# Attention stage of a four-layer transformer block: another written order of the work on all four engines

## The chip, the cores and the metric

The kernel runs on one core of one Trainium2 chip, in one launch. The metric is the device time of the core in microseconds (us), the median of three runs. The engines are PE (TensorE, matrix products; its weight loads are listed as PEld), DVE (VectorE), ACT (ScalarE), POOL (GpSimd) and SP (SyncE, here only the issuing of transfers). Each engine works through its own instructions in the order in which they are written; between engines, semaphores decide.

## The reference

Four layers, each an attention-like part plus a feed-forward-like part on a normalised input, over 4096 rows of 128 values (16 sequences of 256 rows as the kernel lays them out). Only the first layer, called L0 in the kernel, is touched:

```python
# x: 16 sequences x 256 rows x 128;  16 heads of 8
xn = layernorm(x)
q, k, v = heads(xn @ Wq.T + bq), heads(xn @ Wk.T + bk), heads(xn @ Wv.T + bv)
att = softmax(where(causal, q @ k.T / sqrt(8), -inf))
attn = (att @ v) @ Wp.T + bp
ffn = (fp8(xn / s_in) @ fp8(kernel / s_k)) * (s_in * s_k) + bias
x = x + attn + ffn
```

The other layers (a chunked linear attention with a low-rank feed-forward, an attention with a routing tree, a state-space block with six layers of local attention) follow in stages of their own and are the same in both kernels.

## The kernel before

The program has five stages, L0, L1, L2, L3a and L3f, with a barrier of all engines between two of them. L0 works on one sequence of 256 rows at a time, in a software pipeline: the loop at its end runs over rounds k, and in round k each engine runs its list of calls (the last lines of `pe`, `act`, `dve` and `pool`), each call for its own sequence (k - 2 to k + 5). What a list says is the order on that engine. Every call waits by semaphores for its inputs and for its buffers to be free.

For one sequence the steps are: statistics of the rows (`stats`, `moments`, DVE), their logarithm and root (`ln`, `root`, ACT), the normalised rows (`normed`, POOL), turned by PE (`tx`, L299) and copied out by ACT (`xt`). From these PE makes queries and keys (`qk`, L307), which ACT writes out masked by head (`masked`, L489), and values (`vp`, L317), to which DVE adds a bias (`value`). DVE rounds a copy to eight-bit floats in five steps of two instructions (`cast`, `quant` 0 to 4, L191 to L209) for the product of the feed-forward part (`fyp`, L328), which goes on to `scaled` (DVE), `biased`, `ffn` and `keep` (POOL).

The scores of the 16 heads are made twice. In six blocks S0 to S5 (`scores`, L342 to L354) they are made with queries on the partitions, and DVE takes their maxima (`top`, L607, L609). PE turns the maxima (`turn_max`, MX, L366) and DVE lowers the queries by them (`lower`, L629). Then the scores are made again in six blocks T0 to T5 with keys on the partitions (`turned`, L382, L387), ACT takes the exponential (`exponent`, L498), DVE masks (`kept`, L622; 512 elements a partition for blocks 0 to 3, 1024 for 4 and 5), and PE multiplies with the values (`values`, L404, L407). ACT copies the result out (`out`, L507), PE sums (`sl`, L417), ACT takes logarithm and inverse (`logarithm`, `inverse`), POOL multiplies (`shared`, L704), PE projects (`project`, L426) and DVE adds to x (`residual`, L636).

S blocks and T blocks use the PSUM banks 0 to 3 as two pairs in turn, in the fixed order of `RING`: S0, T0, S1, T1, ... S5, T5, MX. So S1 waits until the maximum of S0 has been read, T1 until the exponential of T0 is done, and so on (`wait_pair`). T blocks in round k are of sequence k, S blocks of sequence k + 1. Between two neighbours of this ring other products of PE may stand.

After each round `between` may issue a piece of a later stage's set-up, on whichever engine that needs (`MADE_AT` names the rounds 1 to 7 in which it does for L1, L3a and L3f among others). These instructions stand on each engine behind what the round has issued there and ahead of the next round.

Of the kernel before, what the change touches and what calls it, by code (L numbers as in the profile page):

```python
# [13 lines left out]
NSEQ, SEQ = 16, 256  # L14
# [36 lines left out]
class Kernel:  # L51
# [77 lines left out]
    def L0(self):  # L129
# [152 lines left out]
        def seq(s):  # L282
            return 0 <= s < NSEQ
# [5 lines left out]
        def pe(k):  # L289
# [121 lines left out]
            def sl(s):  # L411
                if not seq(s):
                    return
                p.wait_ge(*o_in.at(s))
                if s:
                    p.wait_ge(*x_done.at(s - 1))
                p.matmul(PS[:, 7, :], lsel[:, :], ob[:, :], start=True, stop=True).then_inc(l_mm.sem)  # L417
# [10 lines left out]

            scores(k + 1, 1)
            turned(k, 1)  # L430
            sl(k - 1)
# [5 lines left out]
            qk(k + 2)  # L437
            scores(k + 1, 4)
            turned(k, 4)
            fyp(k + 1)  # L440
            scores(k + 1, 5)
            turned(k, 5)
            vp(k + 2)
            project(k - 1)
            turn_max(k + 1)
            values(k, 0)
            values(k, 1)
            scores(k + 2, 0)
            turned(k + 1, 0)
            values(k, 2)  # L450

        def act(k):
# [70 lines left out]
            out(k - 1)  # L523
            exponent(k, 1)
            logarithm(k - 1)
            exponent(k, 2)
            xt(k + 2)
            ln(k + 3)
            inverse(k - 1)
            exponent(k, 3)  # L530
            exponent(k, 4)
            root(k + 3)
            masked(k + 2, 0)
            exponent(k, 5)
            masked(k + 2, 1)
            exponent(k + 1, 0)

        def dve(k):
# [98 lines left out]

            quant(k + 1, 4)
            residual(k - 2)
            top(k + 1, 1)  # L640
            kept(k, 0)
            moments(k + 3, 1)
            top(k + 1, 2)
            value(k + 1)
            stats(k + 4, 0)
            kept(k, 1)
            top(k + 1, 3)
            cast(k + 2)
            quant(k + 2, 0)
            stats(k + 4, 1)  # L650
            top(k + 1, 4)
            scaled(k + 1)
            quant(k + 2, 1)
            kept(k, 2)
            top(k + 1, 5)
            quant(k + 2, 2)
            kept(k, 3)
            kept(k, 4)
            quant(k + 2, 3)
            moments(k + 4, 0)  # L660
            lower(k + 1)
            kept(k, 5)
            top(k + 2, 0)

        def pool(k):
# [40 lines left out]
            shared(k - 1)  # L706
            normed(k + 3, 0)
            normed(k + 3, 1)
            biased(k + 1)
            keep(k - 1)  # L710
            ffn(k + 1)
# [14 lines left out]
        for k in range(-2, NSEQ + 2):  # L726
            pe(k)
            act(k)
            dve(k)
            pool(k)  # L730
            self.between(0, k)
# [2553 lines left out]
```

## Time and profile before

| | us |
|---|---|
| runs (median, lowest, highest) | 4755.88, 4755.16, 4768.18 |
| profiled execution, its own time | 4755.88 |
| its span | 4754.6 |
| busy over the span: PE, DVE, ACT, POOL | 4446.8, 3757.2, 3404.6, 3668.2 |
| TensorE's mean granted clock | 0.983 of full speed |

The span is the time from the first to the last instruction of the profile. Busy times are sums over the whole program; L0 is its first 427 us, a little under a tenth. In the timeline an entry merges neighbouring instructions of one line: its start, the time to the end of the last, the operation, and in brackets how long the engine was idle just before and who ended that. Entries of PE overlap by about 0.1 us, since matmuls are pipelined, so the time that a step takes on PE is read from its start to the next start.

### The profile page before, as it was taken

How to read it: one execution, taken by the hardware profiler on the slowest of the kernel's cores; microseconds unless marked ns; L12 is line 12 of the kernel's file. 1: busy time of each engine (PE TensorE's matmuls, PEld its weight loads, DVE VectorE, ACT ScalarE, POOL GpSimd, SP SyncE). 2: the span in 40 equal slices, each digit the busy share in tenths (PEclk: the TensorE clock that was granted, in tenths of full speed). 3: DMA queues.
4: the chain of work that ended last, by engine and by line, in shares of the span. 5: the costliest groups of instructions: out<-in, count | busy, mean ns of one | idle time of the engine just before them, and what ended most of it. 6: DMA issues, size and time to landing. Idle time of an engine off the chain costs nothing.

```text
span 4754.6 us, 138457 instructions
## 1 busy us (share of the span) xinstructions
PE 4446.8 (94%) x56800; PEld 3022.2 (64%) x56800; DVE 3757.2 (79%) x5226; ACT 3404.6 (72%) x6108; POOL 3668.2 (77%) x1951
## 2 busy tenths in 40 slices
PE   7998999988887899999999999999999999999997
PEld 5776778864443566666666666666666666666665
DVE  6885466649998787888778888888888888878885
ACT  3555755547775677777778777877778787777875
POOL 2222344449997998989889999999998999989993
PEclk9999999989999999999999999999999999999999
DMA  2000000003331222223223222232323322322222
GB/s 79 2 2 2 2 1 1 1 39 165 154 143 74 66 67 56 66 73 70 64 57 74 69 66 62 67 73 64 70 61 73 72 58 68 75 67 63 59 66 52
DMA packets 164379, 290.50 MB, mean 61 GB/s; under 512 B 44063, under 2 KB 61350, under 8 KB 159654
## 3 DMA queue, kind: packets, MB, share of 16 engines
q1 hardware_dynamic: 162310, 281.40, 22.7%
q8 instruction: 453, 7.42, 0.7%
q14 instruction: 176, 1.44, 0.1%
q10 hardware_dynamic: 1440, 0.24, 0.0%
HBM read 90.16 MB, written 2.62 MB: 20 GB/s over the span
## 4 chain that ended last, share of the span: by engine, by line
PE 42%; DVE 12%; issue 7%; ACT 5%; POOL 1%; DMA 0%; SPq 0%; ACTq 0%; DVEq 0%; POOLq 0%
PE ps L2562 15%; PE ps L2575 6%; PE ps L2591 5%; PE ps L2618 5%; PE ps L2630 4%; PE ps L2672 3%; PE ps L2604 2%; DVE L3f_sm L2996 2%; DVE ps L2982 2%; DVE L3f_sm L3016 2%; DVE L3f_ss L2955 2%; DVE L3f_raw L2972 1%; DVE L3f_mx L2988 1%; ACT L2779 1%; ACT L3f_gg L2871 1%
## 5 line engine op out<-in xcount | busy, mean ns | idle before, releaser
L3155 POOL TENSOR_TENSOR L3f_t<-L3f_raw,L3f_rot 128x1024 f32<-128x1024 f32 x384 | 999.3, 2603 | 268.3 <-DVE L3f_raw L2972 268.2
L2562 PE MATMUL ps<-L3f_wqkv,all_z 128*128 128x512 f32 x2304 | 1147.0, 607 | 13.4 <-DVE L3f_raw L2972 7.8
L3172 POOL TENSOR_TENSOR L3f_raw<-L3f_raw,L3f_t 128x1024 f32<-128x1024 f32 x384 | 990.4, 2590 | 7.5
L3164 POOL TENSOR_TENSOR L3f_raw<-L3f_raw,L3f_rot 128x1024 f32<-128x1024 f32 x384 | 910.8, 2377 | 15.1
L2972 DVE TENSOR_TENSOR L3f_raw<-ps,L3f_ri 128x512 f32<-128x512 f32 x768 | 498.1, 685 | 287.9 <-ACT L3f_ri L2781 284.9
L2771 ACT ACTIVATE L3f_sqr<-ps 128x512 f32<-128x512 f32 x768 | 453.9, 598 | 174.3 <-PE ps L2562 171.3
L2955 DVE TENSOR_REDUCE L3f_ss<-L3f_sqr 128x8 f32<-128x512 f32 x768 | 509.2, 677 | 74.2 <-ACT L3f_sqr L2771 68.3
L2562 PEld LDWEIGHTS ps<-L3f_wqkv,all_z 128*128 128x128 f32 x2304 | 392.1, 192 | 253.0 <-issue 209.9
L2575 PEld LDWEIGHTS ps<-all_ident,L3f_raw 128*128 128x128 f32 x3072 | 366.6, 141 | 287.0 <-issue 248.5
L2575 PE MATMUL ps<-all_ident,L3f_raw 128*128 128x128 f32 x3072 | 472.1, 276 | 18.2 <-DVE L3f_gg L3038 7.4
L2618 PEld LDWEIGHTS ps<-L3f_pT,L3f_vw 128*64 128x64 f32 x12288 | 378.2, 139 | 97.0 <-issue 90.3
L2618 PE MATMUL ps<-L3f_pT,L3f_vw 128*64 128x64 f32 x12288 | 405.2, 225 | 7.2 <-ACT L3f_pT L2822 5.0
L2822 ACT ACTIVATE L3f_pT<-ps 64x1024 f32<-64x1024 f32 x384 | 389.4, 1014 | 17.2 <-PE ps L2604 12.6
L2805 ACT ACTIVATE L3f_kT<-ps 128x512 f32<-128x512 f32 x384 | 229.4, 597 | 197.9 <-PE ps L2575 194.3
L2630 PE MATMUL ps<-L3f_oT,L3f_wo 128*128 128x256 f32 x1536 | 351.5, 382 | 5.2 <-ACT L3f_oT L2831 3.6
L3016 DVE TENSOR_TENSOR L3f_sm<-L3f_sm,L3f_sl 128x1024 f32<-128x1024 f32 x192 | 348.5, 1815 | 0.1
L2591 PE MATMUL ps<-L3f_kT,L3f_qT 64*32 64x64 f32 x24576 | 300.7, 226 | 50.9 <-issue 37.1
L2591 PEld LDWEIGHTS ps<-L3f_kT,L3f_qT 64*32 64x32 f32 x24576 | 264.4, 105 | 118.3 <-issue 88.5
L2630 PEld LDWEIGHTS ps<-L3f_oT,L3f_wo 128*128 128x128 f32 x1536 | 290.5, 192 | 66.4 <-issue 24.6
L2982 DVE TENSOR_TENSOR ps<-ps,L3f_lmaskb 128x1024 f32<-128x1024 f32 x192 | 235.0, 1224 | 102.8 <-PE ps L2591 102.5
L2281 POOL TENSOR_TENSOR L3a_db_x<-L3a_dx,L3a_Bs 128x1024 f32<-128x1024 f32 x128 | 300.1, 2369 | 1.5 <-DMA L3a_Bs<-L3a_rows 1.3
L2831 ACT ACTIVATE L3f_oT<-ps 128x1024 f32<-128x1024 f32 x192 | 196.1, 1021 | 132.6 <-PE ps L2618 132.6
(335 smaller groups left out, 8883.5 us busy)
## 6 DMA issues: line engine op xcount, KB each, us to landing
L3f_vw<-L3f_v SPq DMA_DIRECT2D x1344, 128.0 KB
L3a_Bs<-L3a_rows SPq DMA_DIRECT2D x16, 2048.0 KB, 7.0
L3a_Cs<-L3a_rows SPq DMA_DIRECT2D x16, 2048.0 KB, 11.7
L3f_vw<-L3f_v SPq DMA_DIRECT2D x192, 64.0 KB
L3f_wqkv<-in_L_ffn_Wqkv SPq DMA_DIRECT2D x24, 256.0 KB, 3.8
L3f_wqkv<-in_L_ffn_Wqkv SPq DMA_DIRECT2D x6, 512.0 KB, 4.3
L3f_wo<-in_L_ffn_Wo SPq DMA_DIRECT2D x48, 64.0 KB
out<-all_x SPq DMA_DIRECT2D x8, 256.0 KB, 3.7
```

Of the source, the lines that this page charges most:

```text
L2562: p.matmul(PS[:, j % 3, :], Z[:, u % NSEQ, t * P:t * P + P], w, start=True, stop=True).then_inc(proj.sem)
L2575: mm = p.transpose(PS[:, 3, c * P:c * P + P], raw[:, t, (4 * g + c) * P:(4 * g + c + 1) * P], ident[:, :])
L2591: mm = p.matmul(PS[w * WIN:(w + 1) * WIN, 6 + h, a * KEYS:(a + 1) * KEYS], qT[r, t, a, w * WIN:(w + 1) * WIN], kT[r, a, t * P + w * WIN:t ...
L2618: mm = p.matmul(PS[to, 4 + c // 2, (c % 2) * 2 * P + w * HD:(c % 2) * 2 * P + (w + 1) * HD], vw[:, u % 2, t * NW + w, a * HD:(a + 1) * HD] ...
L2630: mm = p.matmul(PS[:, 4, 0:SEQ], wo[:, c, h, :], oT[:, :, c, :, h, :], start=(c + h == 0), stop=(c + h == PAIRS // 2))
L2771: a.activation(sqr[:, i % 2, :], PS[:, j % 3, :], ACT.Square).then_inc(sqr_in.sem)
L2955: v.tensor_reduce(ss[:, 0, i * UH:(i + 1) * UH], heads(sqr[:, i % 2, :]), AX.X, ALU.add).then_inc(ss_in.sem)
L2972: v.tensor_tensor(heads(raw[:, t, g * UNIT:(g + 1) * UNIT]), heads(PS[:, RING.index(x) % 3, :]), ri[:, i * UH:(i + 1) * UH].unsqueeze(2).b ...
L3016: v.tensor_tensor(x, x, sl[:, t, :].unsqueeze(2).broadcast_to((P, H, KEYS)), ALU.mult).then_inc(s_mul.sem)
L3155: g.tensor_tensor(t.rearrange("p h (b e) -> p h b e", b=2), r.rearrange("p h (b e) -> p h b e", b=2)[:, :, ::-1, :], w[:, 1, :].rearrange( ...
L3164: g.tensor_tensor(r, r, w[:, 0, :].unsqueeze(1).broadcast_to((P, H, HD)), ALU.mult).then_inc(cosined.sem)
L3172: g.tensor_tensor(r, r, t, ALU.add).then_inc(rotated.sem)
```

## The change

The lists of all four engines in L0 are written in another order, some calls move to another round (`fyp`, `vp`, `scaled`, `biased`, `ffn`, `lower` and the first maxima by one round later in the list, `residual`, `out`, `stats` and one `moments` one earlier), and the loop runs over one round less, since nothing is left for it. No operation is added or taken away, and all waits inside the calls stay.

```diff
@@ -426,28 +426,28 @@
                         mm = p.matmul(PS[:, 7, t * P:(t + 1) * P], on[:, a * SEQ + t * P:a * SEQ + t * P + P], wp[:, a, :], start=(a == 0), stop=(a == 1))
                 mm.then_inc(p_mm.sem)
 
+            fyp(k)
             scores(k + 1, 1)
+            sl(k - 1)
             turned(k, 1)
-            sl(k - 1)
             scores(k + 1, 2)
             turned(k, 2)
             tx(k + 2)
             scores(k + 1, 3)
             turned(k, 3)
-            qk(k + 2)
             scores(k + 1, 4)
+            vp(k + 1)
             turned(k, 4)
-            fyp(k + 1)
             scores(k + 1, 5)
             turned(k, 5)
-            vp(k + 2)
+            qk(k + 2)
+            values(k, 0)
+            values(k, 1)
             project(k - 1)
             turn_max(k + 1)
-            values(k, 0)
-            values(k, 1)
+            values(k, 2)
             scores(k + 2, 0)
             turned(k + 1, 0)
-            values(k, 2)
 
         def act(k):
             a = nc.scalar
@@ -520,20 +520,20 @@
                 a.wait_ge(*l_ln.at(s))
                 a.activation(rl[:, :], rl[:, :], ACT.Exp, scale=-1.0).then_inc(l_inv.sem)
 
-            out(k - 1)
+            exponent(k, 0)
+            ln(k + 3)
+            logarithm(k - 1)
+            root(k + 3)
             exponent(k, 1)
-            logarithm(k - 1)
             exponent(k, 2)
+            exponent(k, 3)
             xt(k + 2)
-            ln(k + 3)
+            exponent(k, 4)
             inverse(k - 1)
-            exponent(k, 3)
-            exponent(k, 4)
-            root(k + 3)
-            masked(k + 2, 0)
             exponent(k, 5)
             masked(k + 2, 1)
-            exponent(k + 1, 0)
+            masked(k + 2, 0)
+            out(k)
 
         def dve(k):
             v = nc.vector
@@ -635,32 +635,32 @@
                 v.wait_ge(*x_kept.at(s))
                 v.tensor_tensor(self.tiles(s), self.tiles(s), PS[:, 7, 0:SEQ].rearrange("p (t d) -> p t d", t=TILES), ALU.add).then_inc(x_done.sem)
 
+            lower(k)
+            top(k + 1, 0)
+            quant(k + 1, 1)
+            quant(k + 1, 2)
+            top(k + 1, 1)
+            quant(k + 1, 3)
+            scaled(k)
+            top(k + 1, 2)
+            kept(k, 0)
+            top(k + 1, 3)
+            kept(k, 1)
+            kept(k, 2)
+            moments(k + 4, 0)
+            top(k + 1, 4)
+            kept(k, 3)
+            value(k + 1)
+            cast(k + 2)
+            top(k + 1, 5)
+            kept(k, 4)
+            kept(k, 5)
+            stats(k + 5, 0)
+            moments(k + 4, 1)
+            residual(k - 1)
+            stats(k + 5, 1)
             quant(k + 1, 4)
-            residual(k - 2)
-            top(k + 1, 1)
-            kept(k, 0)
-            moments(k + 3, 1)
-            top(k + 1, 2)
-            value(k + 1)
-            stats(k + 4, 0)
-            kept(k, 1)
-            top(k + 1, 3)
-            cast(k + 2)
             quant(k + 2, 0)
-            stats(k + 4, 1)
-            top(k + 1, 4)
-            scaled(k + 1)
-            quant(k + 2, 1)
-            kept(k, 2)
-            top(k + 1, 5)
-            quant(k + 2, 2)
-            kept(k, 3)
-            kept(k, 4)
-            quant(k + 2, 3)
-            moments(k + 4, 0)
-            lower(k + 1)
-            kept(k, 5)
-            top(k + 2, 0)
 
         def pool(k):
             g = nc.gpsimd
@@ -703,12 +703,12 @@
                     g.wait_ge(*p_mm.at(s - 1))
                 g.tensor_tensor(on[:, :], ob[:, :], rl[:, :], ALU.mult).then_inc(o_norm.sem)
 
-            shared(k - 1)
+            keep(k - 1)
             normed(k + 3, 0)
             normed(k + 3, 1)
-            biased(k + 1)
-            keep(k - 1)
-            ffn(k + 1)
+            shared(k - 1)
+            biased(k)
+            ffn(k)
 
         self.part.x_done = x_done
         nc.vector.wait_ge(*self.got_x.at(0, 15))
@@ -723,7 +723,7 @@
         nc.gpsimd.wait_ge(*self.got_rest.at(0, 15))
         for engine in (nc.tensor, nc.scalar, nc.gpsimd):
             engine.wait_ge(*w_ready.all(0))
-        for k in range(-2, NSEQ + 2):
+        for k in range(-2, NSEQ + 1):
             pe(k)
             act(k)
             dve(k)
```

On PE, in the middle of a round (S3 and T3, S4 and T4, S5 and T5), the order before is this. L349 with L354 is a score block S, L382 or L387 a T block, L307 queries and keys, L328 the feed-forward product, L317 the values' product, L426 the projection, L366 MX.

```order
L349 MATMUL ps<-L_cmaskb,all_identb 128x2x128 x2
L354 MATMUL ps<-L_km,L_qm 128x256 x4
L382 MATMUL ps<-L_qm,L_km 128x256 x4
L307 MATMUL ps<-L_xnT,L_wt 128x256 x2
L349 MATMUL ps<-L_cmaskb,all_identb 128x2x128 x2
L354 MATMUL ps<-L_km,L_qm 128x256 x4
L387 MATMUL ps<-L_qm,L_km 128x128 x8
L328 MATMUL ps<-L_kq,L_xq 128x128 x2
L349 MATMUL ps<-L_cmaskb,all_identb 128x2x128 x2
L354 MATMUL ps<-L_km,L_qm 128x256 x4
L387 MATMUL ps<-L_qm,L_km 128x128 x8
L317 MATMUL ps<-L_wt,L_xnT 128x128 x2
```

The same place after the change, from T3 on:

```order
L382 MATMUL ps<-L_qm,L_km 128x256 x4
L349 MATMUL ps<-L_cmaskb,all_identb 128x2x128 x2
L354 MATMUL ps<-L_km,L_qm 128x256 x4
L317 MATMUL ps<-L_wt,L_xnT 128x128 x2
L387 MATMUL ps<-L_qm,L_km 128x128 x8
L349 MATMUL ps<-L_cmaskb,all_identb 128x2x128 x2
L354 MATMUL ps<-L_km,L_qm 128x256 x4
L387 MATMUL ps<-L_qm,L_km 128x128 x8
L307 MATMUL ps<-L_xnT,L_wt 128x256 x2
L404 MATMUL ps<-L_pT,L_vz 32x256 x16
L426 MATMUL ps<-L_wp,L_on 128x128 x4
L366 MATMUL ps<-L_nident,L_mxe 128x128 x8
```

The queries' and keys' product has left the place between T3 and S4 for one behind T5; the values' product stands between S4 and T4; the feed-forward product has gone to the start of the round, between T0 and S1.

On DVE, around the lowering of the queries (L629), with the piece of a later stage's set-up that is issued after round 3 (L1787 to L1793), before:

```order
L555 BN_AGGR L_ln_mv<-L_ln_st 128x2
L629 TENSOR_TENSOR L_qm<-L_qm,ps 128x1024
L622 SCALAR_TENSOR_TENSOR L_pT<-L_pT,L_keep 128x1024
L607 TENSOR_REDUCE L_mxe<-ps 128x2x2 x2
L1787 TENSOR_TENSOR L3a_cbr<-L3a_cbr,L3a_cbp 128x256
L1789 TENSOR_SCALAR L3a_dg<-all_ident,L3a_dd 128x128 x2
L1791 CAST L3a_cbp<-L3a_cbr 128x256
L1793 TENSOR_SCALAR L3a_na<-L3a_na 128x32
```

and after the change, from the masks of blocks 4 and 5 on:

```order
L622 SCALAR_TENSOR_TENSOR L_pT<-L_pT,L_keep 128x1024 x2
L546 BN_STATS L_ln_st<-all_x 128x6
L555 BN_AGGR L_ln_mv<-L_ln_st 128x2
L636 TENSOR_TENSOR all_x<-all_x,ps 128x256
L546 BN_STATS L_ln_st<-all_x 128x6
L207 TENSOR_TENSOR L_qz_w<-L_qz_w 128x256
L209 TENSOR_TENSOR L_xq<-L_qz_r,L_qz_w 128x256
L191 TENSOR_SCALAR L_qz_p<-L_xb,L_rsc 128x256
L193 TENSOR_SCALAR L_qz_m<-L_qz_p 128x256
L1787 TENSOR_TENSOR L3a_cbr<-L3a_cbr,L3a_cbp 128x256
L1789 TENSOR_SCALAR L3a_dg<-all_ident,L3a_dd 128x128 x2
L629 TENSOR_TENSOR L_qm<-L_qm,ps 128x1024
```

The inserted piece and the end of the quantiser now stand ahead of L629, where before L629 and the first maxima (L607) came first.

## Rows read from the trace of the kernel before

**Rows 1.** Stretches: start:end us, length, busy us of engines (instructions), PEclk, DMA share, GB/s

```profile
200.00:250.00 50.00, 48.95 (x507) 35.70 (x508) 43.15 (x78) 26.57 (x45) 13.36 (x13) 1.00 0.01 2
```

**Rows 2.** Timeline of PE over one round: start us, us, operation, [idle before <-releaser]

```profile
217.07 0.60 PE L342 MATMUL ps<-L_cmaskb,all_identb 128*128 128x512 bf16 x2
...
223.38 0.38 PE L349 MATMUL ps<-L_cmaskb,all_identb 128*128 128x256 bf16 x2 [0.19 <-DVE L_mxe L609]
...
226.59 0.38 PE L349 MATMUL ps<-L_cmaskb,all_identb 128*128 128x256 bf16 x2
...
228.85 0.28 PE L328 MATMUL ps<-L_kq,L_xq 128*128 128x128 bf16 x2
229.45 0.38 PE L349 MATMUL ps<-L_cmaskb,all_identb 128*128 128x256 bf16 x2 [0.31 <-DVE L_mxe L609]
...
230.73 1.06 PE L387 MATMUL ps<-L_qm,L_km 32*128 32x128 f32 x16
231.71 0.71 PE L317 MATMUL ps<-L_wt,L_xnT 128*128 128x128 f32 x4
232.26 1.06 PE L426 MATMUL ps<-L_wp,L_on 128*128 128x128 f32 x8
233.15 1.95 PE L366 MATMUL ps<-L_nident,L_mxe 128*128 128x128 f32 x16
235.03 1.93 PE L404 MATMUL ps<-L_pT,L_vz 128*32 128x256 f32 x32
236.90 0.61 PE L342 MATMUL ps<-L_cmaskb,all_identb 128*128 128x512 bf16 x2
...
238.43 1.03 PE L382 MATMUL ps<-L_qm,L_km 32*128 32x256 f32 x8
239.39 1.08 PE L407 MATMUL ps<-L_pT,L_vz 128*32 128x128 f32 x32
240.41 0.60 PE L342 MATMUL ps<-L_cmaskb,all_identb 128*128 128x512 bf16 x2
```

**Rows 3.** Timeline of PE, S2 of the first counted round

```profile
80.17 0.38 PE L349 MATMUL ps<-L_cmaskb,all_identb 128*128 128x256 bf16 x2
```

**Rows 4.** Timeline of PE, S2 and S3 of the last round with scores

```profile
383.94 0.38 PE L349 MATMUL ps<-L_cmaskb,all_identb 128*128 128x256 bf16 x2
...
386.81 0.38 PE L349 MATMUL ps<-L_cmaskb,all_identb 128*128 128x256 bf16 x2 [0.56 <-DVE L_mxe L609]
```

**Rows 5.** Timeline of DVE in the round of rows 2

```profile
222.01 1.23 DVE L609 TENSOR_REDUCE L_mxe<-ps 128x4 f32<-128x1024 f32 x1 [1.22 <-PE ps L354]
...
236.59 1.19 DVE L629 TENSOR_TENSOR L_qm<-L_qm,ps 128x1024 f32<-128x1024 f32 x1
237.69 1.22 DVE L622 SCALAR_TENSOR_TENSOR L_pT<-L_pT,L_keep 128x1024 f32<-128x1024 f32 x1
...
240.03 0.41 DVE L207 TENSOR_TENSOR L_qz_w<-L_qz_w 128x256 f32<-128x256 f32 x1
```

**Rows 6.** Timelines of DVE and POOL one round earlier

```profile
206.93 0.68 DVE L622 SCALAR_TENSOR_TENSOR L_pT<-L_pT,L_keep 128x512 f32<-128x512 f32 x1
...
209.89 2.83 DVE L622 SCALAR_TENSOR_TENSOR L_pT<-L_pT,L_keep 128x512 f32<-128x512 f32 x2
...
210.52 1.12 POOL L689 TENSOR_TENSOR all_x<-all_x,L_yb 128x256 f32<-128x256 f32 x1
```

**Rows 7.** Timeline of DVE after round 2, an inserted instruction

```profile
123.22 1.22 DVE L1784 TENSOR_TENSOR L3a_wc<-L3a_wi,L3a_cwr 128x1024 f32<-128x1024 f32 x1
```

**Rows 8.** Timelines of ACT and PE at the head of L0

```profile
17.67 0.30 ACT L461 ACTIVATE L_ln_ls<-L_ln_mv,all_eps 128x2 f32<-128x2 f32 x1 [2.63 <-DVE L_ln_mv L555]
...
22.00 1.01 PE L342 MATMUL ps<-L_cmaskb,all_identb 128*128 128x512 bf16 x2 [3.98 <-ACT L_km L489]
```

**Rows 9.** Timeline of POOL at the end of L0

```profile
423.63 1.26 POOL L704 TENSOR_TENSOR L_on<-L_ob,L_rl 128x512 f32<-128x512 f32 x1 [3.88 <-ACT L_rl L521]
424.85 0.73 POOL L695 TENSOR_TENSOR all_x<-all_x,L_bvp 128x256 f32<-128x256 f32 x1
```

## What was predicted

> **What bounds the kernel now.** The change touches only the first of five stages, L0. I read first the table of stretches: between 200 and 250 us TensorE (PE) is busy 48.95 of 50 us at a granted clock of 1.00 (the full 2.4 GHz), DVE 43.15, ACT 26.57, POOL 13.36 [rows 1]. So the stage is set by PE, with DVE not far behind. The barrier after L0 ends at about 427 us; nothing after it is reordered, so the question is how long L0 takes.
>
> Then the PE timeline of one round [rows 2]. Let S0 to S5 be the six score blocks (a mask product, L342 or L349, then L346 or L354), T0 to T5 the six transposed blocks (L382, L387), MX the turned maxima (L366). The round runs from S1 at 217.07 to S1 at 240.41: 23.34 us. PE waits in it twice, 0.19 and 0.31 us, each time at the start of a score block and each time for DVE's maximum (L609) of the score block before it, because both use the same pair of PSUM banks. The other 22.84 us are PE's own work, which the change leaves alone. That bounds the gain: 0.50 us a round. The counted rounds run from S2 at 80.17 [rows 3] to S2 at 383.94 [rows 4]: 303.77 us, 13 rounds. At best 13 x 0.50 = 6.5 us come back.
>
> How far apart must two score blocks be? The last round has a place where only one T block lies between two of them: S2 starts at 383.94, S3 at 386.81, idle 0.56 [rows 4]. A score block takes 1.28 (229.45 to 230.73, rows 2), so from its end to the next start pass 2.87 - 1.28 = 1.59 us. This is 0.2 until DVE starts, 1.23 of L609 [rows 5], 0.15 back to PE. It is a floor: whatever PE has between two score blocks is free up to 1.59, and missing filler is waited out. S0's maximum is read in two halves and I take 1.60 for it.
>
> **The change part by part.** No arithmetic is added; what moves is the filler. Start to start, from rows 2: T (238.43 to 239.39) 0.96, the later T4 and T5 0.99, qk 226.59 - 223.38 - 1.28 - 0.96 = 0.97, fyp 0.28 (row 228.85), vp 0.55, project 0.89, MX 1.88, first values 1.87, last values (239.39 to 240.41) 1.02, S0 1.53.
> - S0 to S1. Before: T0 and last values, 1.98, no wait. Now T0 and fyp, 1.24: wait 0.36.
> - S1 to S2: T1 and the sum product (L417), no wait in either order.
> - S2 to S3: T2 and the turning of x (L299, L300), unchanged, wait 0.19.
> - S3 to S4. Before T3 and qk, 1.93. Now T3 alone, 0.96: wait 0.63. This is the largest term.
> - S4 to S5. Before T4 and fyp, waits 0.31. Now vp and T4, 1.54: wait 0.05.
> - S5 to MX: T5, qk, first values and project, 4.72 instead of 2.43. MX needs the last maximum 1.6 after S5; covered in both.
> Waits per round: 0.36 + 0.19 + 0.63 + 0.05 = 1.23 against 0.50. That is +0.73, a period of 24.06; 13 rounds give 9.5 us. PE's groups may cost 0.1 more or less a round in new company: bound 8 to 11.
>
> Next, whether DVE arrives in time. With S1 starting at 0, S2 starts at 3.45, S3 6.31, S4 9.17, S5 12.03, MX 18.0, the next S0 20.9, T0 22.45, the next S1 24.05. The maxima begin at about 1.7, 4.9, 7.8, 10.7, 13.5, and 22.6 for the next S0. Between them the small operations fit, the tightest with about 0.3 us to spare (keep-masks of blocks 1 and 2 before the maximum of S4). After the maximum of S5 (free at 14.7) come the two 1024-wide masks (L622, 1.22 each or 1.13 start to start, rows 5), three short statistics, the residual, four quantiser steps (L207 took 0.41, rows 5, and none of the eight passes 0.45; I take 2.35 for them together) and the lowering L629 (1.19, or 1.10 start to start, rows 5), which T0 waits for. Alone: 14.7 + 2.26 + 2.35 + 1.10 = 20.4, and not before MX ends at 19.9. But POOL's four tensor_tensors now stand in one run: the shared product starts when ACT's inverse, queued behind exponent 4, ends (about 13.7), then bias, ffn, keep. L622 is slowed beside them. In the round shown one 512-wide and one 1024-wide mask took 2.83 beside POOL [rows 6]; alone they take 0.68 [rows 6] and 1.22 [rows 5]: 0.93 lost in the 1.75 us from 209.89 to the end of POOL's L689 at 211.64, so DVE works at 0.47 of its pace. L689 took 1.12 there [rows 6], and L695 of the same size takes 0.73 alone [rows 9], so POOL works at 0.65. Together 1.12, that is, both need 0.89 of what one after the other would. Now 2.26 of DVE's work meets about 2.4 of POOL's: 4.66 x 0.89 = 4.15, so the masks end near 18.8, the short ones near 21.2, L629 near 22.3. T0 wants it at 22.45 and may slip to 22.8 before S1 slips, since fyp and T0 lie inside the 1.60. So DVE has about 0.5 us left: nothing is added per round, but DVE is nearly as tight as PE.
>
> The Trainium skill ("SBUF — State Buffer", section "Who interferes with whom") says that a DVE instruction with two SBUF inputs and a GpSimd instruction that reads SBUF contend, and that the second to start blocks fully. The trace has the contact but a little less than full blocking: 0.89, worked out above, where full blocking gives 1. By full blocking the masks would end at 19.3 and L629 at 22.8, which leaves nothing to spare and is the seed of the second case below.
>
> That matters for what the set-up of later stages inserts. After each of six early rounds DVE gets foreign work; the longest single one is L1784, 1.22 us [rows 7], and the six lots are about 0.45, 1.3, 1.0, 1.4, 0.15 and 0.8. Before, they stood behind S0's maximum, ahead of slack. Now they stand behind the quantiser and directly ahead of L629. With 0.5 of cover they cost 0 + 0.8 + 0.5 + 0.9 + 0 + 0.3 = 2.5; with no cover 5.1. I take 3.
>
> Head. S0 of sequence 0 starts at 22.00, having waited for ACT's masks; these stood behind the logarithm at 17.67, which ACT had idled 2.63 us to get [rows 8]. Now the statistics come one round earlier and logarithm and root precede, so the masks start right after qk (its products end near 17.1): about 1.0 earlier. But qk of sequence 1 has moved from before S4 to after S5, and its masks (two times 1.9) are then wanted by the next S0 about 0.8 after MX ends. Together -0.3. PE runs here at the lower clock and idles a little more than before, so the rise to full speed may come later, by 0 to 3 us of time: I take +1, hence +0.7. The first, partly filled round comes out at 22.8 in both.
>
> Tail. Before, MX to T0 took 1.88 + 1.87. In the last rounds T0 has to wait for L629 with first values already done: from S5's end 7.05 to T0 instead of 5.73, +1.3. At the very end the shared product (before at 423.63, rows 9) stands behind the next stage's first normalisation and one keep: +0.4. Together +1.7, bounds 0.5 and 2.5.
>
> **Sum.** The profiled execution took 4755.88, which is the median itself, span 4754.6. 9.5 + 3 + 0.7 + 1.7 = 14.9: 4770.8, taken as 4771. Low bound 8 + 2 - 0.3 + 0.5 = 10, 4766; high bound 11 + 5.1 + 3 + 2.5 = 21.6, 4777.
>
> **The rivals.**
> Second case, DVE becomes the bound. Full blocking leaves no cover: about 0.1 a round (1.3) and the whole 5.1 of inserted work: 9.5 + 1.3 + 5.1 + 0.7 + 1.7 = 18.3, 4774. If the 512-wide masks meet POOL as well, half a microsecond a round more, 4781. For it: 43.15 of 50 us busy [rows 1] and the late quantiser. Against: 0.5 us of cover by the walk above, and PE's own floor of 24.05 is reached first.
>
> Third case, PE's waits are only partly paid. Should the head gain stay whole (-1), the insertions hide (1) and neighbouring groups pack 0.1 better (8.2), 8.2 + 1 - 1 + 0.5 = 9: 4765. For it: at S2 to S3 nothing changes. Against: the tail's own row with 0.56.
>
> Fourth case, on the other side, not slower. One mechanism: the freed DVE order delivers the maximum of S3 before T3 ends, and then no filler is needed. It decides at 0.96 us after S3; then the two old waits vanish too and 13 x 0.5 = 6.5 us are gained: 4749. For it: the maximum of S5 is no longer followed by MX at once. Against: 1.23 of L609 alone [rows 5] is more than 0.96, and the wait for the bank pair is in the code.
>
> **How the numbers follow.** No change and change can be told apart by about 0.3%, 14 us: above 4770.1 counts as slower, below 4741.6 as faster. Forecast 0.50 (own range 4766 to 4777), second case 0.25, third 0.18, fourth 0.05, and 0.02 for something not thought of that gains. Slower: 0.3 of the forecast's 0.50, as 4771 lies at the line, plus 0.24 of the second: 0.54. Faster by over 0.3% 0.02, since no case gains 14 us. Same: 0.44. The range leaves out the fourth case and the end of the second: 4762 to 4782.
>
> **What would show it.** In the profile after: a round of 24.05 us in L0; L349 idle twice near 0.6 and 0.2, L342 at S1 idle near 0.3, all for L609 or L607; L622's 1024-wide form above 1.22; in the rounds with inserted DVE work a wait of T0 (L382) for L629. Wrong: a round at or above 24.5 with PE waiting for L629 in each (second case), or under 23.6 (fourth); a head or tail that moves by more than 3 us.

## The result, and the profile after

The changed kernel is slower. Its five runs have a median of 4795.81 us (4789.11 to 4804.49), the five runs of the kernel before, taken beside them, 4764.87 (4755.16 to 4769.08): ratio 1.0076, with a 95% interval of 1.0055 to 1.0095. The forecast of 4771 us, range 4762 to 4782, was too low by 25 us; as a difference, 14.9 us were forecast and 30.9 measured between the two medians. The side, slower, was right, and most of the reason was not.

The profiled execution took 4792.03 us, its span 4790.6 against 4754.6. The first product of PE in the next stage (L811) starts at 471.80 instead of 427.1, 44.7 later, so the loss lies in L0. What follows L0 is 8.7 shorter in this execution; its length differs by up to 10.7 between executions of one and the same kernel. Three profiled executions of each kernel give 428.7 and 472.1 on the mean (+43.4) and spans of 4751.1 and 4795.5 (+44.4).

First the 280 us in the middle of L0, in the table of stretches of the kernel before; the columns are length, busy us and count of PE, PEld, DVE, ACT and POOL, then PE's granted clock:

```profile
100.00:380.00 280.00, 273.91 (x2899) 199.25 (x2896) 240.14 (x420) 143.96 (x240) 70.66 (x72) 1.00 0.01 2
```

The same view of the kernel after, with a stretch at full clock and three short ones:

```profile
100.00:380.00 280.00, 269.59 (x2522) 184.23 (x2514) 206.70 (x373) 127.28 (x208) 68.95 (x64) 0.93 0.01 1
370.00:420.00 50.00, 47.90 (x488) 33.09 (x486) 37.82 (x61) 24.25 (x38) 12.08 (x10) 1.00 0.01 2
175.00:180.00 5.00, 4.02 (x38) 2.19 (x30) 4.74 (x12) 1.65 (x3) 0.00 (x0) 0.88 0.01 3
180.00:185.00 5.00, 5.00 (x23) 3.13 (x24) 2.58 (x6) 0.84 (x3) 0.00 (x0) 0.50 0.00 0
...
210.00:215.00 5.00, 5.00 (x70) 4.17 (x68) 3.29 (x9) 1.48 (x3) 0.00 (x0) 1.00 0.00 0
```

Two things show. PE's granted clock is no longer 1.00 throughout: from about 179 us to a little ahead of 210 it is 0.50, which is 1.2 GHz, with PE busy 5.00 of 5. And at full clock PE is busy 47.90 of 50, where it was 48.95 [rows 1].

Now a round at full clock, PE's timeline after, against [rows 2] (start, time to the end of the last, operation, and in brackets the idle time just before):

```profile
396.38 0.59 PE L342 MATMUL ps<-L_cmaskb,all_identb 128*128 128x512 bf16 x2 [0.40 <-DVE L_mxe L607]
396.90 1.16 PE L346 MATMUL ps<-L_km,L_qm 32*128 32x128 f32 x16
397.99 1.13 PE L417 MATMUL ps<-L_ob,L_lsel 128*128 128x512 f32 x2
399.05 1.13 PE L382 MATMUL ps<-L_qm,L_km 32*128 32x256 f32 x8
400.12 0.39 PE L349 MATMUL ps<-L_cmaskb,all_identb 128*128 128x256 bf16 x2
...
402.99 0.38 PE L349 MATMUL ps<-L_cmaskb,all_identb 128*128 128x256 bf16 x2
...
405.85 0.38 PE L349 MATMUL ps<-L_cmaskb,all_identb 128*128 128x256 bf16 x2 [0.56 <-DVE L_mxe L609]
...
407.22 0.71 PE L317 MATMUL ps<-L_wt,L_xnT 128*128 128x128 f32 x4
407.86 1.16 PE L387 MATMUL ps<-L_qm,L_km 32*128 32x128 f32 x16
408.96 0.39 PE L349 MATMUL ps<-L_cmaskb,all_identb 128*128 128x256 bf16 x2
...
410.25 1.15 PE L387 MATMUL ps<-L_qm,L_km 32*128 32x128 f32 x16
411.33 1.13 PE L307 MATMUL ps<-L_xnT,L_wt 128*128 128x256 f32 x4
412.39 1.93 PE L404 MATMUL ps<-L_pT,L_vz 128*32 128x256 f32 x32
414.25 1.16 PE L426 MATMUL ps<-L_wp,L_on 128*128 128x128 f32 x8
415.25 1.95 PE L366 MATMUL ps<-L_nident,L_mxe 128*128 128x128 f32 x16
...
418.14 0.60 PE L342 MATMUL ps<-L_cmaskb,all_identb 128*128 128x512 bf16 x2
...
421.32 0.59 PE L342 MATMUL ps<-L_cmaskb,all_identb 128*128 128x512 bf16 x2 [0.40 <-DVE L_mxe L607]
```

The round is 421.32 - 396.38 = 24.94 us, not 24.06. The two large waits are where the forecast put them, 0.40 ahead of S1 and 0.56 ahead of S4; the two small ones of the forecast, ahead of S3 and S5, are not there. The idle times are together 0.96 where they were 0.50. What a wait costs is read from start to start: S3 takes 1.27 and T3 0.96, and S4 starts 2.86 after S3, so that wait costs 0.63; the one of 0.19 in the kernel before cost 0.09. In this way the waits cost 0.63 a round more than before, and the other 0.97 of the 1.60 are longer blocks. Against the walk of the prediction, from start to start:

| stretch | walked | measured | between the two |
|---|---|---|---|
| S1 to S2 | 3.45 | 3.74 | S1 1.61, L417 1.06, T1 1.07 instead of 1.53, 0.96, 0.96 |
| S2 to S3 | 2.86 | 2.87 | T2 1.06, and the wait of 0.19 is gone |
| S3 to S4 | 2.86 | 2.86 | the walked floor holds |
| S4 to S5 | 2.86 | 3.11 | S4 1.37, vp 0.64, T4 1.10 |
| S5 to S0 | 8.87 | 9.18 | T5 1.08, qk 1.06, project 1.00 |
| S0 to S1 | 3.15 | 3.18 | wait 0.40 instead of 0.36 |

In the three stretches with a wait in the forecast, the two differ by 0.03 at most. The whole gap of 0.88 a round sits in the other three, which were taken to be free of waits or nearly so: there the nine blocks named in the table are 0.1 longer each (T2 is the tenth).

What a longer block looks like from the side of the weight loads: of the kernel before, T2 in [rows 2], whose first product starts at 221.80,

```profile
221.59 0.84 PEld L382 LDWEIGHTS ps<-L_qm,L_km 32*128 32x128 f32 x8
```

and T1 and T2 of the kernel after, whose first products start at 244.76 and 247.12:

```profile
244.76 0.73 PEld L382 LDWEIGHTS ps<-L_qm,L_km 32*128 32x128 f32 x8 [0.76 <-issue]
...
247.08 0.76 PEld L382 LDWEIGHTS ps<-L_qm,L_km 32*128 32x128 f32 x8 [0.20 <-issue]
```

Before, the first load runs 0.21 ahead, while the score block still multiplies. After, it starts with the block. For T1 the sum product L417 now stands just ahead, for T2 the exponential of block 1 ends at that moment, since the logarithm of the sums has been put in front of it. The Trainium skill ("TensorE: Matmul & The Clock Gate", "The mechanism") says that PE pulls weight loads ahead of matmuls in flight where they do not conflict. The row of before shows such a load, those of after show two that were not pulled; what stops them in T1 no run here settles.

Last the place where the clock falls, DVE and then PE of the kernel after:

```profile
175.67 0.71 DVE L1801 COPY L3a_bb<-L3a_cbp 1x256 bf16<-1x256 bf16 x3
176.41 1.22 DVE L629 TENSOR_TENSOR L_qm<-L_qm,ps 128x1024 f32<-128x1024 f32 x1
```

```profile
177.78 1.13 PE L382 MATMUL ps<-L_qm,L_km 32*128 32x256 f32 x8 [0.98 <-DVE L_qm L629]
...
179.03 1.06 PE L342 MATMUL ps<-L_cmaskb,all_identb 128*128 128x512 bf16 x2
180.02 2.08 PE L346 MATMUL ps<-L_km,L_qm 32*128 32x128 f32 x16
182.03 2.08 PE L417 MATMUL ps<-L_ob,L_lsel 128*128 128x512 f32 x2
```

A later stage's set-up (L1801) stands ahead of L629 on DVE, as forecast, and T0 waits 0.98 for it. From 179.03, 1.25 us after PE has resumed, every operation takes twice its time: L346 2.08 instead of 1.16, L417 2.08 instead of 1.13.

The rounds, as distances between the starts of L417. Before: 13 of 23.33 to 23.57, then 19.96 and 18.19 of the last, partly empty ones. After: 24.94, 25.08, 24.94, 27.07, 36.74, five of 24.94, 29.59, 24.94, 24.94, then 20.81 and 21.02. The 44.7 us are therefore 13 x (24.94 - 23.34) = 20.8; the long stretch at half clock, with some 0.7 of the wait ahead of it, 27.07 + 36.74 - 2 x 24.94 = 13.9; a short one, 29.59 - 24.94 = 4.7; the head 0.8 (first L417 at 80.00 against 79.21); the tail 4.8 (48.87 against 44.12); and -0.3 of small differences.

### The profile page after: what moved, and what is told of

Same layout as the page of the kernel before. It is cut to its first block, busy times and chain, and to the rows that moved or that the text cites. A ratio compares the mean times of both kernels' runs of the same rounds, so it can differ in the third digit from the quotient of the medians.

```text
span 4790.6 us, 138456 instructions
## 1 busy us (share of the span) xinstructions
PE 4473.7 (93%) x56800; PEld 3026.4 (63%) x56800; DVE 3758.3 (78%) x5226; ACT 3405.2 (71%) x6108; POOL 3681.0 (77%) x1951
## 4 chain that ended last, share of the span: by engine, by line
PE 42%; DVE 12%; issue 7%; ACT 5%; POOL 1%; DMA 0%; SPq 0%; ACTq 0%; DVEq 0%; POOLq 0%
PE ps L2562 15%; PE ps L2575 6%; PE ps L2591 5%; PE ps L2618 5%; PE ps L2630 4%; PE ps L2672 3%; PE ps L2604 2%; DVE L3f_sm L3016 2%; DVE L3f_sm L2996 2%; DVE ps L2982 2%; DVE L3f_ss L2955 2%; DVE L3f_raw L2972 1%; DVE L3f_mx L2988 1%; ACT L2779 1%; ACT L3f_gg L2871 1%
## 5 line engine op out<-in xcount | busy, mean ns | idle before, releaser
L2562 PE MATMUL ps<-L3f_wqkv,all_z 128*128 128x512 f32 x2304 | 1146.4, 607 | 14.9 <-DVE L3f_raw L2972 9.5
```

Source lines behind the costliest of these rows:

```text
L2562: p.matmul(PS[:, j % 3, :], Z[:, u % NSEQ, t * P:t * P + P], w, start=True, stop=True).then_inc(proj.sem)
```

## The experiments

Theory A was that a block is 0.1 longer where its first weight load does not overlap the block before it, and that putting the old neighbours back gives these tenths back; theory B was that the round is longer because DVE or the bank waits come late. Theory C was that one long wait of PE brings the half clock; theory D, that such stretches come here and there with a PE stream that has more waits. The usual round length repeats to 0.02 in every profiled execution; a time by itself is one run, unless said otherwise, and single times of the kernel before differ by up to 29 us on one chip, so the readings go by the rounds.

**Two neighbourhoods undone in the changed kernel.** First the sum product and the logarithm:

```diff
             scores(k + 1, 1)
-            sl(k - 1)
             turned(k, 1)
+            sl(k - 1)
@@ act
+            exponent(k, 1)
             logarithm(k - 1)
             root(k + 3)
-            exponent(k, 1)
```

> The changed kernel with the sum product (L417) back behind T1, and ACT's logarithm behind exponent 1. Round of the changed kernel: 24.94 us at full clock. Theory A (a group of fp32 products shows about 0.1 us of its first weight load, unless it is a T block directly behind its S block with its wait already over; and the moved fillers have broken these neighbourhoods): S1, L417 and T1 lose 0.08 + 0.10 + 0.11, so the round becomes 24.65. Rival B (the 0.9 us over the forecast 24.06 is DVE or the bank waits arriving late): these groups keep their length and the round stays at 24.9.

Measured: 24.64 a round, 0.30 less than 24.94, as A said. S1, L417 and T1 take 1.52, 0.96 and 0.96. T2 is short again too (0.96), although its neighbours on PE are the same in all these kernels; only the exponential of block 1 on ACT now ends 1.1 us ahead of it instead of in the same moment. So there are two causes of a longer block: its neighbours, and an input that comes just in time. The time was 4787.45 beside 4754.76 of the kernel before on that chip. T0 waited 0.97 in round 4 again, and no stretch at half clock followed; one came at round 13 (30.92), and the first L417 came only at 85.25.

Then vp behind T4, and the copy xt behind exponent 4:

```diff
-            vp(k + 1)
             turned(k, 4)
+            vp(k + 1)
@@ act
-            xt(k + 2)
             exponent(k, 4)
+            xt(k + 2)
```

> The changed kernel with the values' product (L317) back behind T4 instead of ahead of it, and ACT's copy xt behind exponent 4. Theory A: S4 takes 1.28 instead of 1.37, S4's end to S5 falls from 1.73 to 1.59 and T5 from 1.08 to 0.98: the round becomes about 24.6. Rival B: S4 to S5 is already set by DVE's maximum, so the round stays at 24.9.

Measured: 24.59, 0.35 less; which of the two moved calls gives which tenth is not separated here. The time was 4807.68: a long stretch (27.18, 36.05), two short ones (29.40, 29.41), and the first L417 only at 87.40.

Both together, timed four times:

> Both of the edits before on the changed kernel. Theory A: they add, 24.94 - 0.29 - 0.33 = 24.32 us a round, and 13 x 0.62 = 8 us less than the changed kernel in L0 at full clock. Rival B: 24.9.

Measured: 24.28, so the two gains add (0.66). PE's timeline shows what became short again, S1 and L417 among them:

```profile
293.22 1.16 PE L346 MATMUL ps<-L_km,L_qm 32*128 32x128 f32 x16
294.21 1.03 PE L382 MATMUL ps<-L_qm,L_km 32*128 32x256 f32 x8
295.18 1.12 PE L417 MATMUL ps<-L_ob,L_lsel 128*128 128x512 f32 x2
296.14 0.38 PE L349 MATMUL ps<-L_cmaskb,all_identb 128*128 128x256 bf16 x2
...
299.00 0.38 PE L349 MATMUL ps<-L_cmaskb,all_identb 128*128 128x256 bf16 x2 [0.19 <-DVE L_mxe L609]
```

T1 takes 0.97 and L417 0.96, and the old wait of 0.19 ahead of S3 is back, since S2 and T2 no longer fill it. Yet the time was 4791.76 (4787.42 to 4794.98, four runs), ratio to the kernel before 1.0081, 1.005 to 1.0113: the 13 x 0.66 = 8.6 us do not show (the changed kernel had 1.0076), and the profiled run had the long stretch (26.65, 34.49) and a late first L417 (88.19).

**One more of the moves, alone and in the kernel before.** qk from ahead of S4 to behind T5, with its first masks behind exponent 5:

```diff
-            qk(k + 2)
             scores(k + 1, 4)
             turned(k, 4)
             fyp(k + 1)
             scores(k + 1, 5)
             turned(k, 5)
+            qk(k + 2)
@@ act
-            masked(k + 2, 0)
             exponent(k, 5)
+            masked(k + 2, 0)
```

> The kernel before with one filler moved alone: queries' and keys' product (L307) from between T3 and S4 to behind T5, and its masks on ACT behind exponent 5. The forecast's largest term: S3's end to S4 falls from 1.93 to the floor of 1.59 while the 0.97 of L307 is now paid behind T5, +0.63; theory A adds 0.09, since L307 is followed by L317 there and no longer by a bf16 mask product: 23.34 + 0.72 = 24.06 us a round. Rival B: 23.34 + 0.63 = 23.97. Theory D (a PE stream with more waits falls to half clock now and then): half-clock stretches between 100 and 400 us, of which the kernel before showed none in one look.

Measured: 23.86 a round, +0.52, and 4775.27 beside 4757.18. Both expectations, 24.06 of theory A and 23.97 of B, were too high. The waits are 0.19, 0.56 and 0.31; of the rows, the longest wait and the end of the round:

```profile
254.21 0.38 PE L349 MATMUL ps<-L_cmaskb,all_identb 128*128 128x256 bf16 x2 [0.56 <-DVE L_mxe L609]
...
259.34 1.13 PE L307 MATMUL ps<-L_xnT,L_wt 128*128 128x256 f32 x4
260.30 0.61 PE L317 MATMUL ps<-L_wt,L_xnT 128*128 128x128 f32 x4
260.75 1.06 PE L426 MATMUL ps<-L_wp,L_on 128*128 128x128 f32 x8
```

So this one move costs one more wait of 0.56, which is 0.62 from start to start, as forecast (0.63), and gives 0.10 back because vp behind qk, which is of its kind, takes 0.45 instead of 0.55. The 0.09 that theory A added for qk did not come: qk takes 0.96 (259.34 to 260.30). One stretch at half clock (29.83) came here too.

**Was the half clock chance?** The same two kernels again, unchanged:

> The kernel before once more, for the half-clock stretches. Theory D: rounds of 23.34 and no or hardly any stretch at half clock between 100 and 400 us, and the first L417 again near 79 us. Rival E (they come by chance, in either kernel alike): one or more here too.

> The changed kernel once more. Rounds of 24.94 at full clock. Theory C (a fixed cause, the 0.98 us wait of T0): the long stretch again from about 179 us. Theory D: one or more stretches, not at the same places. Rival E: as often none.

Measured: 4756.31, L811 at 431.9, all 13 rounds at full clock; but in the last round with scores the clock fell, which the other two profiles of the kernel before do not show, and L0 ended 4.9 later for it. That round, here as in [rows 4], waits 0.56:

```profile
389.80 0.38 PE L349 MATMUL ps<-L_cmaskb,all_identb 128*128 128x256 bf16 x2 [0.56 <-DVE L_mxe L609]
...
393.18 2.08 PE L354 MATMUL ps<-L_km,L_qm 32*128 32x256 f32 x8
```

The changed kernel: 4794.27, L811 at 464.8, T0's wait 0.97, then 26.96 and 36.91. Both later once more, on another chip:

> The kernel before, third look: rounds of 23.34 and no half-clock stretch between 100 and 385 us, whatever theory holds; one there would speak for chance.

> The changed kernel, third look. Theory C: the wait of T0 behind round 4, 0.98 us in both looks so far, has the long stretch behind it again, in most though not in all looks (of all variants with the changed order 6 of 8 had it). Short stretches of about 5 us at changing places.

Measured: 4745.09, L811 at 427.0, no such stretch; and 4804.42, L811 at 479.6, T0's wait 0.96, then 26.13 and 36.10, a short one (31.23), and the first L417 at 87.77. So in three profiled executions of three the changed kernel has the long stretch behind round 4, and in none of three the kernel before has one in its 13 rounds.

**Taking away what T0 waits for.** `lower` at the end of DVE's list, ahead of the set-up that is inserted there:

```diff
-            lower(k)
             top(k + 1, 0)
...
             quant(k + 2, 0)
+            lower(k + 1)
```

> The changed kernel with DVE's lowering (L629) of the next sequence at the end of the round's list, ahead of the inserted set-up work instead of behind it. Forecast step: T0's wait for L629 in the round with three L1801 copies (0.98 us in the changed kernel) goes; the round at full clock stays 24.94 us. Theory C (the half-clock stretch from 179 to 209 us in the changed kernel followed from this wait): no stretch at half clock between 100 and 400 us near that place. Rival D (such stretches come with the sparser PE stream, wherever they fall): a half-clock stretch in L0 all the same, or at another place; in the changed kernel there was a second one at 353 to 363 us with only the usual waits ahead of it.

Measured: 24.94 as before, 4779.25. The wait did not go, it moved to S1, whose pair of banks is freed by a maximum that now stands behind the set-up:

```profile
184.24 0.59 PE L342 MATMUL ps<-L_cmaskb,all_identb 128*128 128x512 bf16 x2 [1.08 <-DVE L_mxe L607]
```

No long stretch followed, and a short one came late (29.59); the first L417 came at 85.29. Once more the same kernel:

> The changed kernel with the lowering ahead of the inserted work, a second look. Theory C: PE's wait behind round 4 is now split in another way (1.08 us at S1 in the first look), and no long stretch began there; if the long stretch follows any wait of 1 us, it may come this time. Theory D: short stretches at other places than in the first look.

Measured: 4795.29. This time the clock fell at about 168 us, in the round of 31.91, behind nothing but the usual waits of 0.40 and 0.56. S1 waited 1.08 again, at 190.06, some 8 us after the clock had come back, and no stretch followed; a short one came in the last of the 13 rounds (29.58). The short time of the first run is thereby not shown to be due to `lower`.

**A wait made on purpose in the kernel before.** DVE takes two maxima over 1024 unused elements at the start of rounds 5, 8 and 11, later three in rounds 8, 10 and 12 (all line numbers shift by 3):

```diff
+            if k in (5, 8, 11):
+                for n in range(2):
+                    v.tensor_reduce(dlo[:, ...], dly[:, :], AX.X, ALU.max)
             quant(k + 1, 4)
```

> The kernel before with three long waits put into PE's stream: at the head of DVE's list in rounds 5, 8 and 11 two maxima over 1024 elements of a buffer of their own (about 1.1 us each start to start, their results unused), which make the maximum of S1 late and let PE wait at S2 about 1 us. Theory C (one wait of about 1 us is enough to lose the full clock): a half-clock stretch directly behind each of the three, each costing some 5 to 14 us, in a kernel that showed none between 100 and 385 us in two looks. Rival F (the wait alone does nothing, it is the changed kernel's other waits around it): three rounds longer by about 1 us, no stretch.

Measured: 4773.3. In round 5, where set-up work stands there too, PE waited 2.20, and 25.61 and 34.06 followed, at half clock until about 201 us. In rounds 8 and 11 it waited 0.66 and 0.67, less than the 1 us that was expected: 24.07 and 23.57, and no stretch, so there theory C was not put to the test.

```profile
175.08 1.10 PE L420 MATMUL ps<-L_ob,L_lsel 128*128 128x512 f32 x2 [2.20 <-DVE all_x L639]
```

> The kernel before with three maxima over 1024 unused elements at the head of DVE's list in rounds 8, 10 and 12, where nothing of the set-up is inserted. In b_wait two of them gave a wait of 0.66 us and no stretch, and together with set-up work 2.20 us and a stretch of 26 us. Three give about 1.8 us each. Theory C (a single long wait loses the clock): a half-clock stretch behind each of the three, 10 us and more each. Rival F (the stretches belong to the time near 175 us or to the set-up work): three rounds of 25.1, no stretch.

Measured: 4787.88 beside 4744.60. The three waits are 1.80, 1.95 and 1.79 us, and each is followed by the half clock; the table of stretches shows full speed ahead of one and half behind all three:

```profile
246.25 1.10 PE L420 MATMUL ps<-L_ob,L_lsel 128*128 128x512 f32 x2 [1.80 <-DVE all_x L639]
...
305.75 2.05 PE L420 MATMUL ps<-L_ob,L_lsel 128*128 128x512 f32 x2 [1.95 <-DVE all_x L639]
...
366.27 1.37 PE L420 MATMUL ps<-L_ob,L_lsel 128*128 128x512 f32 x2 [1.79 <-DVE all_x L639]
```

```profile
240.00:245.00 5.00, 4.45 (x68) 2.99 (x64) 5.00 (x7) 2.13 (x3) 0.00 (x0) 1.00 0.01 3
255.00:265.00 10.00, 10.00 (x50) 7.06 (x48) 5.04 (x10) 2.14 (x3) 1.21 (x2) 0.50 0.01 2
310.00:320.00 10.00, 10.00 (x40) 6.45 (x38) 4.68 (x10) 3.02 (x5) 1.26 (x1) 0.50 0.00 0
370.00:380.00 10.00, 10.00 (x42) 6.39 (x40) 4.29 (x8) 3.02 (x5) 1.26 (x1) 0.50 0.00 1
```

The pairs of rounds are 25.21 + 34.03, 25.47 + 35.33 and 25.19 + 33.78, that is 12.3 to 14.1 over 2 x 23.34, of which the wait itself is under 2. With the 2.20 (13.0 over) that is four of four.

**All three undone at once, and one more.** The sum product, vp and `lower` together:

> The changed kernel with the three undone parts together: sum product behind T1, values' product behind T4, lowering ahead of the inserted work. Theory A: 24.28 us a round as with the first two. Theory C: no long half-clock stretch behind round 4, since the round loses only about 0.7 us there; short ones of some 5 us may remain. L0 then ends some 14 us earlier than in the looks with the stretch, and the time is about 4775.

Measured: 24.28, but 4792.10 (4778.98 to 4832.74, eight runs), ratio 1.0094, 1.0061 to 1.0127. The expected 4775 was missed by 17 us in the median, and the expected absence of the long stretch was wrong: S1 waited 1.08 in round 4, and 27.13 and 35.51 followed. The profiled execution is the fastest of the eight all the same (4778.98): its L0 ends 32.3 us later than that of the kernel before, and what follows L0 is 9.2 shorter. What slowed the slowest of the eight, which were not profiled, is not known.

On top of it `project` ahead of the first values:

> e7_all with the projection (L426) ahead of the first values (L404) instead of behind them. Theory A: two groups of 128 rows and 128 columns (L307, L426) then stand together and one change of kind is gone: 24.28 - 0.1 = 24.18 us a round. Rival G (the remaining 0.24 us are latencies of DVE and ACT, not PE's neighbours): 24.28 as before.

Measured: 24.28, not 24.18, and 4775.09 in one run, with two short stretches (30.64 and 29.07) and no long one; S1's wait in round 4 was 0.83. The expectation was miscounted: qk takes 0.97 (272.39 to 273.36) and project 0.98 (to 274.34), but MX behind the values takes 1.99 (276.20 to 278.19) instead of 1.88: the tenth moved to the next change of kind.

**The other way, from the kernel before.** fyp goes behind tx and vp behind T4, so that no score block lacks filler, with `scaled` and `value` earlier on DVE:

```diff
             tx(k + 2)
+            fyp(k + 1)
...
             turned(k, 4)
-            fyp(k + 1)
+            vp(k + 2)
             scores(k + 1, 5)
             turned(k, 5)
-            vp(k + 2)
```

> The kernel before, with two fillers moved into the two bank waits that it has: the feed-forward product (L328) behind the turning of x, between T2 and S3, and the values' product (L317) between T4 and S5; on DVE value one place earlier and scaled directly behind the maximum of S3. By the floor of 1.59 the waits of 0.19 and 0.31 go but for 0.05, all groups keep their neighbours in kind (each filler directly ahead of a bf16 mask product): 23.34 - 0.45 = 22.89 us a round, 13 x 0.45 = 5.8 us in all, about 0.12%, which the timed runs hardly tell. Rival: DVE comes too late for one of the maxima, the round stays at 23.3 or more.

Measured: 23.14, not 22.89, and 4752.22 (twelve runs) beside 4757.18, ratio 0.9993, 0.998 to 1.0005. The rival, a round of 23.3 or more, did not come either. Both waits of [rows 2] are gone, but project takes 0.1 more, and S0 now waits for ACT, which writes the key masks too late:

```profile
258.25 1.96 ACT L489 ACTIVATE L_km<-ps,L_bm,L_mask 128x256 f32<-128x256 f32 x4
```

They end at 260.21, and S0 starts at 260.30, 2.07 after the first values instead of 1.87. In the last round with scores, where this kernel waits 0.56 too, the clock fell here as well, at about 391 us. None of the kernels tried is measurably faster than the one before.

## Why the prediction was wrong

- **The cover of a score block, 1.59, and the waits at S1 and S4.** Right: 0.40 and 0.56 idle, 0.41 and 0.63 from start to start, for 0.36 and 0.63, and the distances S3 to S4 and S0 to S1 came out within 0.03.
- **"The other 22.84 us are PE's own work, which the change leaves alone."** This is the first step that failed. Ten blocks are 0.1 longer each in the new order, 0.97 a round. The term "13 rounds give 9.5" is 20.8, of which 13 x 0.63 = 8.2 is waits and 13 x 0.97 = 12.6 is longer blocks. The bound of 0.1 a round for "new company" was the price of one block, and ten were changed; undoing two of the moves took back 0.66.
- **The inserted set-up.** The place was right (T0 waits for L629 behind L1801) and, as wait, the price was too high: round 2 is 0.14 longer, and round 4, in the two variants where no half clock followed (e1_sl and e4_lower), 0.68 (25.32 - 24.64) and 0.67 (25.61 - 24.94): about 0.8 us, not 3. The second failure is that only the wait was priced. The half clock behind it cost 12 to 13 more, and between 100 and 380 us of three executions of the kernel before the clock never fell. In the three profiled executions of the changed kernel, stretches at half clock in the 13 rounds cost 18.6, 14.0 and 18.6 us, nearly as much as the longer rounds.
- **The second case, DVE as the bound.** It did not come: apart from round 4 no wait of a full-clock round is for L629, and those for maxima have the size of the undelayed path. The two masks beside POOL took 3.06 where 4.15 had been worked out:

```profile
232.37 3.06 DVE L622 SCALAR_TENSOR_TENSOR L_pT<-L_pT,L_keep 128x1024 f32<-128x1024 f32 x2
```

```profile
231.47 1.27 POOL L704 TENSOR_TENSOR L_on<-L_ob,L_rl 128x512 f32<-128x512 f32 x1 [5.80 <-ACT L_rl L521]
232.69 1.66 POOL L681 TENSOR_TENSOR L_yb<-L_yb,L_fbias 128x256 bf16<-128x256 bf16 x1
234.42 1.53 POOL L689 TENSOR_TENSOR all_x<-all_x,L_yb 128x256 f32<-128x256 f32 x1
```

  The contact is there (3.06 against 1.14 + 1.22 = 2.36 alone, and L689 1.53 against the 0.73 of L695, which is of its size), but the masks began when L704 was nearly done.
- **Head, +0.7.** In the execution of the first profile +0.8, but by luck. S0 of the first sequence starts at 21.99 and not 1.0 earlier, the clock does not rise later, and the next S0 starts at 51.51 instead of 50.76, because it waits 1.32 for ACT's masks. Over three executions it is +2.9, because the first L417 came at 78.59 and 87.77 in the other two. The 87.77 (a_again2) is not a later rise of the clock but a second fall, which the forecast did not have; the clock had risen by 51 us and was at half again from about 58 to 78:

```profile
57.36 0.38 PE L349 MATMUL ps<-L_cmaskb,all_identb 128*128 128x256 bf16 x2 [0.62 <-DVE L_mxe L607]
...
59.24 1.92 PE L382 MATMUL ps<-L_qm,L_km 32*128 32x256 f32 x8
```

  In 6 of 10 profiled executions of kernels with the changed order the head has this second fall, and the first L417 comes at 84.8 or later; in the seven of the kernel before and its variants it has none (79.1 to 80.7).
- **Tail, +1.7.** 47.8 to 48.9 in three executions against 44.1, 48.8 and 44.1; the 48.8 is the one in which the clock fell in the last round. Against the other two it is +4.4 on the mean; the bound was 2.5. In the first profile the part from S5's end to T0 is +1.65 (forecast 1.3), the last S blocks take 1.4 more, which the forecast had left out, and the rest is 1.7 (forecast 0.4).

The waits and the set-up's place were read off rows and hold. The failures are both of one kind: PE's time was taken as a sum of fixed durations, independent of what stands next to a block and of the clock.

What stays open is when exactly the clock falls. Waits of 1.8 to 2.2 us were followed by the half clock four times of four (in one of them it fell 0.2 us before the wait ended). T0's or S1's wait of 0.96 to 1.08 in round 4 was followed by it in six profiled executions of nine. Short stretches, behind none but the usual waits, cost 4.6 to 7.0 us each. In the 13 rounds there were 11 of them, in 8 of the 11 profiled executions of kernels that wait 0.56 in each round, the single move of qk among them, and in none of the six of kernels that do not.

The traces show one thing more, which the experiments did not set out to test: where these stretches begin. All 11 begin within 2.6 us of the end of a wait of 0.56, in rounds of 24 to 25 us. The two of b_again1 and e6_fyp_vp begin 2.3 and 2.6 us behind one, in the only round in which these kernels wait 0.56. The second falls in the head begin within 1.5 us of the end of a wait of 0.62 or 0.56; the kernel before has the 0.62 there too (at 57.09) and no fall. That speaks for these waits as the occasion. It does not say why about one such wait in thirteen brings the half clock and the others do not (waits of 0.66 and 0.67 did not, but there were only two), and no run took the wait away and left the rest. The Trainium skill ("TensorE: Matmul & The Clock Gate", "A second HAM failure mode: psum-queue depth-cycling") tells of a kernel whose small idle times between groups of matmuls make the clock swing between its two levels. The short stretches look like that, in a kernel where most waits are also for PSUM banks.

## What to carry to other kernels

A reordering on a saturated PE is not priced by its waits alone: count every place where the neighbours of a block change kind, or where the input of a block arrives just in time, and put 0.1 us on each (here ten a round, more than the new waits cost). Where PE runs at full clock, treat each new wait of about 1 us as one that can cost ten times its length, and one of 0.56 in each round as one that now and then costs 5 to 7 us, above all where rarely executed work is inserted in front of an instruction that PE waits for. Read the granted clock in more than one profiled execution before saying what an order costs.

## What the runs showed of the hardware

- The first weight load of a block runs 0.2 us ahead, beside the block before it, in some orders and not in others (seen for L382); blocks take 0.1 longer in some places than in others (L382 0.96 or 1.06, L307 0.96 or 1.06, L426 0.89 or 1.00, L366 1.88 or 1.99, L317 0.45 behind L307 and 0.55 to 0.64 elsewhere).
- Single waits of PE of 1.79 to 2.20 us, behind more than 100 us at full clock or some 34 us after the last such stretch, were each followed by 24 to 27 us at 1.2 GHz, in which PE was busy without a gap where it was measured (10.00 of 10.00): 12 to 14 us lost for each, wait included.
- Short stretches at 1.2 GHz (4.6 to 7.0 us lost) began within 2.7 us of the end of a wait of 0.56, in 13 cases of 13; most waits of 0.56 brought none.
- Two DVE masks of 1024 elements beside POOL took 3.06 from the first start to the last end, where twice the one alone is 2.36: 1.22, of which 1.14 to the next start (237.69 to 238.83) [rows 5].
